# Moving the point at which VectorE's batch loop turns round, in a four-layer graph network kernel

## The reference, cut to what matters

```python
# layer 0
h = relu(layernorm(x));  agg = epsilon * h + adj @ h
x = x + silu(rmsnorm(agg @ W1 + b1) * rms_weight) @ W2 + b2
# layer 1
h = relu(layernorm(x)) @ W.T + b
att = sigmoid(s1[:, None] + s2[None, :] + att_b) * adj * mask * mask.T
x = x + (att / (att.sum(-1) + 1e-8)) @ h * mask
# layer 2: 8 heads, softmax(q @ k.T / sqrt(32) + adj * W_e, where adj != 0) @ v, then @ W_o.T
# layer 3
h = relu(layernorm(x));  x = x + (d[:, None] * adj * d[None, :]) @ (h @ weight) + bias,  d = (adj.sum(-1) + 1e-5) ** -0.5
```

## Time and profile before

| what | before |
|---|---|
| median of 3 runs, us | 4106.58 |
| lowest and highest, us | 4103.77, 4110.3 |
| span of the profiled execution, us | 4105.1 |
| TensorE busy (matmul) | 3772.7 us, 92% |
| VectorE busy | 2585.8 us, 63% |
| ScalarE busy | 2302.1 us, 56% |
| GpSimd busy | 688.4 us, 17% |
| mean granted TensorE clock | 0.986 |
| DMA engines busy with data | 25.3% |

### The profile page before, as it was taken

How to read it: one execution, slowest core, us unless ns; L and a number is a source line. 1 busy time by engine, 2 the same in 40 slices (tenths; PEclk the granted TensorE clock), 3 DMA queues, 4 the chain that set the end, 5 groups by cost and what they waited for, 6 DMA issues and landing times.

```text
span 4105.1 us, 69147 instructions
## 1 busy us (share of the span) xinstructions
PE 3772.7 (92%) x20364; PEld 2683.0 (65%) x20364; DVE 2585.8 (63%) x6404; ACT 2302.1 (56%) x5155; POOL 688.4 (17%) x1483
## 2 busy tenths in 40 slices
PE   4899999999999999999999999999999999999997
PEld 3666666666666666766666666667666666666674
DVE  3666666666666666666666666666666666666664
ACT  2555565555665555665555655556655556555564
POOL 1121111111111211111121111121111211111110
PEclk9999999999999999999999999999999999999999
DMA  2232222222222322222222223222223222232212
GB/s 73 57 83 62 64 70 61 73 77 67 62 61 62 82 62 68 65 67 66 79 65 62 61 62 82 62 72 61 72 62 82 62 62 61 62 82 66 72 47 62
DMA packets 166933, 275.03 MB, mean 67 GB/s; under 512 B 23906, under 2 KB 59874, under 8 KB 166756
## 3 DMA queue, kind: packets, MB, share of 16 engines
q1 hardware_dynamic: 166756, 273.45, 25.3%
HBM read 122.37 MB, written 16.78 MB: 34 GB/s over the span
## 4 chain that ended last, share of the span: by engine, by line
PE 60%; issue 19%; DVE 11%; ACT 5%; POOL 4%; DVEq 0%; SPq 0%; DMA 0%; POOLq 0%; ACTq 0%
PE turn L1114 9%; PE value L1129 6%; PE front L929 5%; PE front L931 5%; PE front L930 5%; PE score L1104 4%; PE score L1105 4%; PE front L1039 3%; PE front L1024 3%; PE score L1147 3%; PE front L981 3%; POOL small L342 2%; PE score L1161 2%; DVE small L792 2%; DVE hid L719 2%
## 5 line engine op out<-in xcount | busy, mean ns | idle before, releaser
L536 ACT ACTIVATE prob<-prob,small 128x512 f32<-128x512 f32 x1024 | 736.3, 719 | 446.5 <-DVE small L815 445.2
L815 DVE CUSTOM_DVE_ANT_0 prob<-score,adj_sb,drv 128x512 f32<-128x512 f32 x1024 | 761.8, 747 | 250.0 <-PE score L1105 240.4
L1114 PE MATMUL turn<-ident,prob 128*128 128x128 f32 x4096 | 617.2, 276 | 14.1 <-ACT pT L545 8.3
L1114 PEld LDWEIGHTS turn<-ident,prob 128*128 128x128 f32 x4096 | 484.0, 141 | 135.7 <-issue 45.7
L545 ACT ACTIVATE pT<-turn 128x512 f32<-128x512 f32 x768 | 447.1, 585 | 140.7 <-PE turn L1114 140.6
L1104 PE MATMUL score<-qk_stack 128*128 128x512 f32 x1024 | 486.9, 479 | 20.7 <-DVE small L815 19.1
L1105 PE MATMUL score<-unlinked,neg_mask 128*128 128x512 bf16 x1024 | 399.8, 390 | 0.0
L929 PE MATMUL front<-w_hi,s_hi 128*128 128x256 f32 x1024 | 352.2, 344 | 28.5 <-DVE x_in L732 28.5
L442 ACT ACTIVATE hb<-x,small 128x256 f32<-128x256 f32 x256 | 132.8, 589 | 355.7 <-POOL small L346 355.7
L931 PE MATMUL front<-w_hi,s_lo 128*128 128x256 f32 x1024 | 287.4, 281 | 0.0
L930 PE MATMUL front<-w_lo,s_hi 128*128 128x256 f32 x1024 | 286.8, 280 | 0.0
(11 more groups left out here) (137 smaller groups left out, 7515.7 us busy)
## 6 DMA issues: line engine op xcount, KB each, us to landing
qk_stack<-qk SPq DMA_DIRECT2D x1024, 128.0 KB, 2.4
adjT_f<-in_adjT SPq DMA_DIRECT2D x32, 1024.0 KB, 5.4
adj_sb<-in_adj SPq DMA_DIRECT2D x32, 1024.0 KB, 7.9
prob<-in_adjT SPq DMA_DIRECT2D x32, 1024.0 KB, 5.3
x_in<-in_x SPq DMA_DIRECT2D x32, 512.0 KB, 3.5
out<-x_out SPq DMA_DIRECT2D x32, 512.0 KB, 3.0
pT<-in_W SPq DMA_DIRECT2D x2, 1024.0 KB
rmsw_b<-in_rmsw SPq DMA_DIRECT2D x1, 512.0 KB
```

What stands on the lines that cost most here:

```text
L536: act.activation(prob[:, i % 8, :], prob[:, i % 8, :], ACT.Exp, bias=nmax[:, h, n:n + 1], scale=-1.0, accum_out=prsum[:, h, n:n + 1]).then ...
L815: dve.tensor_tensor_reduce(out=prob[:, i % 8, :], in0=SB_[i % 2][:, :], in1=adj_sb[:, n, :], scale=neg_w[:, h:h + 1], scalar=3e38, op0=ALU ...
L1114: last = pe.transpose(TB[k % 2][:, tile(n)], prob[:, (4 * h + n) % 8, tile(j)], ident[:, :])
```

## The change

`phases` of VectorE is cut in two behind `diagonal`: `opening(t, tf)` holds `turned`, `stats0` and `diagonal`, `rest(t, tf)` all that follows. The loop's body now begins with `rest(t, t + 1)` and ends with `opening(t + 1, t + 2)`. VectorE issues the same steps in the same order for the same batches as before. Its loop runs 29 times (t = 1 to 29) instead of 30; one more opening stands in front of the loop, and one more `rest` behind it. The other engines' programs stay as they are.

```diff
-            def phases(t, tf):
+            def opening(t, tf):
                 b, f = t is not None, tf is not None
                 if b:
                     turned(t, 0, 0)
                 if f:
                     stats0(tf)
                     diagonal(tf)
+
+            def rest(t, tf):
+                b, f = t is not None, tf is not None
                 if b:
                     qk_low(t, 0, 0)
                     qk_low(t, 0, 1)
...
-            phases(None, 0)
-            phases(0, 1)
-            with dve.Fori(1, B - 1) as t:
-                phases(t, t + 1)
-            phases(B - 1, None)
+            opening(None, 0)
+            rest(None, 0)
+            opening(0, 1)
+            rest(0, 1)
+            opening(1, 2)
+            with dve.Fori(1, B - 2) as t:
+                rest(t, t + 1)
+                opening(t + 1, t + 2)
+            rest(B - 2, B - 1)
+            opening(B - 1, None)
+            rest(B - 1, None)
```

## The result

The changed kernel takes 4037.94 us in the median (4036.79 to 4039.34, 4 runs), the kernel before 4105.90 us (4103.77 to 4110.30) beside it: a ratio of 0.9832 with a 95% interval of 0.9818 to 0.9846 (the two medians divided give 0.9834). Forecast: 4037 us. The profiled execution took 4037.71 us with a span of 4035.9 us, so what lies around the span is 1.8 us.

What follows compares the result with a forecast made beforehand. TensorE, busy 92%, idled at each batch boundary for VectorE's copy, late by the loop's 2.8 us return. Span 4105.1 - 69.7 (29 stretches becoming like batch 1) = 4035.4, plus 1.48 to the median's scale: 4037 us, range 4030 to 4048.

Steps and rivals of the forecast that it cites:

- The hole: VectorE's idling before its copy of the turned rows is the loop's 2.8 us return, in all 29 returns.
- Batch 1 as the control: Batch 1, run in front of the loop without a return, takes 122.82 us; the 29 others should become like it.
- top-down sum: All 29 stretches between last updates become like batch 1: 3631.43 - 29 x 122.82 = 69.7 us gained.
- The clock: Half-rate TensorE stretches after the 3.1 us boundary idling vanish with it: 20 x 0.44 = 8.8 us.
- rival A: Half-rate stretches stay or return elsewhere, so only 63.6 us of idle time is gained: 4043 us; chance 0.18.
- bottom-up sum: 63.6 us of VectorE's idle time before the copy plus 8.8 us for the clock, 72 us.
- The cover: Behind diagonal VectorE idles 4.14 us before the q remainder, so the 2.8 us return there costs nothing.
- Rival B: Return behind diagonal grows to 5.6 us, 0.8 over the cover: 22 us given back, about 4059 us; chance 0.06.
- C: Three return waits in a row behind diagonal, 8.4 us, 3.6 over the cover: +37 us, about 4144; chance 0.02.
- The 108 ns rule: Skill's compare-and-branch price: VectorE's 29 returns would cost 3 us in all, so no change, 4104 us.

Runs made afterwards that it cites:

- e1: The kernel before with 72 sequencer instructions without effect at the start of VectorE's program, order of work unchanged: 4036.04 us, ratio 0.9822 to the kernel before.
- e11: The changed kernel with a useless 2.3 us reduction in front of VectorE's copy of the turned rows, every batch but the first: 4100.42 us, ratio 0.9975.
- e3: The changed kernel with 48 instructions without effect at the start of VectorE's program, which made its return short (0.27 us): 4035.82 us, ratio 0.9824.
- e12: The changed kernel with one useless reduction behind diagonal and a wait for its end in front of the branch: 4035.52 us, ratio 0.9817.
- e5: The changed kernel with the return moved forward to between VectorE's copy of the turned rows and stats0: 4183.38 us, ratio 1.0178.
- e6: The changed kernel with VectorE's return moved forward to between stats0 and diagonal: 4023.63 us, ratio 0.9789.
- e4: The changed kernel with 30 instructions without effect at the start of ScalarE's program, making its return slow: 4040.21 us, ratio 0.9833.
- e8: The changed kernel with two useless reductions behind diagonal, without a wait for their end: 4035.15 us, ratio 0.9818.

## Why the prediction was right

**The hole is the return, and it costs what it delays.** Right: copy, TensorE's wait and the 2.8 us of the branch came out as forecast to 0.1 us. e1 is the strongest evidence, since it takes the return away and leaves the order of the work alone.

**Batch 1 as the control.** Right: the 29 stretches became 122.88 us for the control's 122.82. That one row carried the number; the top-down sum of 69.7 us came out as 67.9 in the profiled execution, and as 68.0 between the medians. That it came so near is in part luck: in the changed kernel the stretch of batch 1 itself takes 123.02 us, and 0.2 us of scatter in the one row that is multiplied by 29 is 6 us.

**The clock.** Right that the half-rate segments go with the idling, which rival A doubted; e11 shows that the link is idling. Of the 67.9 us gained, 8.7 are the clock's: the mean over all 29 stretches was 125.22 us before and 124.92 over those at full clock, 29 x 0.30. The other 59.2 are the idle time (29 x 2.04), for 63.6 in the bottom-up sum; in e1, where a full-clock stretch took 122.71, it was 29 x 2.21 = 64. In the changed kernel the copy did come 2.19 us earlier behind the last update (3.06 to 0.87 us), as the sum had it, but the stretch became only 2.04 us shorter; the 0.15 us per batch between the two stay open, like the 0.18 us that e3 showed.

**The cover.** Right in its result, wrong in one sentence: "each return would have to last over 4.8 us to cost anything". e12 showed a return that ends 5.9 us behind L694's start and costs nothing. The step that failed is taking the q remainder for a part of the chain that sets the batch; that chain runs over the statistics, GpSimd, hf and the aggregate (e5), and the remainder has between 1.1 and 2.0 us of its own. Rival B's 22 us were priced too high by the same error, since an overrun of 0.8 us would have vanished; so was C's.

**What I didn't see.** In the timeline read for the forecast, GpSimd's L342 takes 1.02 us for hb and 1.52 beside VectorE's diagonal:

```profile
1996.90 1.02 POOL L342 TENSOR_TENSOR small<-small,drv 128x4 f32<-128x4 f32 x1
...
2006.59 1.52 POOL L342 TENSOR_TENSOR small<-small,drv 128x4 f32<-128x4 f32 x1
```

I shifted the whole stretch as one block and never asked whether it was as short as it could be; the change leaves those 0.6 us per batch lying, and moving the return one step further to the front (e6) picks them up by accident.

**The 108 ns rule** (the Trainium skill, Advanced Engine Details and Errata, Control Flow Timing) is nearest where the return is short: 0.16 us for GpSimd, 0.26 for ScalarE, 0.27 for VectorE in e1, from the branch to the body's first row. Even there the measured times are one and a half to two and a half times the rule's. Where packets come behind the branch it is off by far: 2.8 us for VectorE, 2.4 for ScalarE in e4.

## What to carry to other kernels

Where a hardware loop's return stands alone on a critical wait ("issue" before the first instruction of the body), there are two cures: turn the loop round where that engine waits for another anyway, or place the body so that it stays held; an iteration written out in front of the loop is the control that tells in advance what either is worth. Look at what follows the wait, not only at the waiting instruction: one step too early (e5) the same move cost 75 us instead of gaining 68. And look for instructions of GpSimd that last longer beside VectorE's than alone.

## What the runs showed of the hardware that I had not expected

- 72 instructions without effect made this kernel 1.8% faster; 24 did nothing. Any edit to the code in front of such a loop can move its time by that much, so comparing unrelated edits of it is unsafe unless the loop's return is looked at in both traces.
- In e8 VectorE's sequencer ran ahead of 4.5 us of reductions and made its return beside them; in e12 a wait for the reduction's own result held the branch back until it had ended.
- The half-rate clock raised the price of a 3 us stall: in e5, 28 returns of 3.4 us cost 145 us, 5.2 us each.
- Open: why the return took 3.4 us in e5 (an output store is issued just before that branch, at 2040.83, but no run separates it).
